# Cross-attention and a routed mixture of experts on one core: weight pieces, early loads, and where the empty tiles stand

## The reference

```python
x = x + xattn(layernorm(x), ctx, Wq, Wg, bg, Wkv, Wo)
#   q = fm(query @ Wq.T), k = fm(kv @ Wk.T), v = kv @ Wv.T, 16 heads; fm(t) = t+1 if t>0 else exp(t)
#   kv_summary = sum over s of k v^T, z = 1/(q . k_sum + eps)
#   out = (q kv_summary z) * sigmoid(query @ Wg.T + bg) @ Wo.T
x = x + ffn(layernorm(x), Wr, We, be)
#   logits = x @ Wr (8 experts); top 2, softmax over the two
#   out = sum over experts e of gate_e * (x @ We[e] + be[e])
```

## Time and profile before

| what | us |
|---|---|
| median of three timed runs | 557.02 |
| the profiled execution, its own time | 559.25 |
| its span, from first to last instruction | 557.7 |
| first 100 us: start, keys and queries of batch 0 | 100 |
| three like stretches of 97 us (to 391.3) | 291.3 |
| expert tiles and the tail | 166.4 |

### The profile page before, as it was taken

One profiled execution on the slowest core, in us unless ns is written; L12 is line 12 of the kernel. 1 busy time (PEld: TensorE's weight loads), 2 busy tenths in 40 slices (PEclk: granted clock), 3 DMA queues, 4 the chain that ended last, 5 costly groups with the idle time before them and its releaser, 6 DMA issues.

```text
span 557.7 us, 12238 instructions
## 1 busy us (share of the span) xinstructions
PE 523.0 (94%) x4084; PEld 424.3 (76%) x4084; DVE 305.6 (55%) x918; ACT 209.7 (38%) x372; POOL 211.8 (38%) x235
## 2 busy tenths in 40 slices
PE   6999999899999999999999999999998879998990
PEld 5777788687778888777887878788876658886880
DVE  4483248637533773753377375377677675443440
ACT  6455432343443234344323444432442234333330
POOL 5342346521566032256603125300133563544353
PEclk9999999999999999999999999999999989999996
DMA  8912943551464225146422513679897988756855
GB/s 265 392 60 79 300 143 130 187 196 74 138 209 134 93 81 203 60 141 206 148 78 96 202 46 119 214 261 365 278 274 232 256 166 167 153 105 116 167 68 65
DMA packets 40873, 92.93 MB, mean 167 GB/s; under 512 B 4784, under 2 KB 4784, under 8 KB 40688
## 3 DMA queue, kind: packets, MB, share of 16 engines
q0 software_dynamic: 15184, 42.56, 28.7%
q1 hardware_dynamic: 24336, 47.22, 25.4%
q10 hardware_dynamic: 1296, 2.40, 1.3%
HBM read 53.81 MB, written 40.18 MB: 169 GB/s over the span
## 4 chain that ended last, share of the span: by engine, by line
PE 55%; DMA 16%; issue 7%; POOL 4%; POOLq 3%; DVE 1%; ACTq 1%; ACT 1%; DVEq 0%
PE pj L1133 15%; PE pj L1135 15%; PE pj L1134 15%; DMA out_dram<-khat,out_idx 8%; DMA out_dram<-buf,out_idx 6%; PE tp L1125 5%; PE pj L1220 2%; PE kvb L1192 2%; POOL aux L517 1%; DMA wraw<-in_L_ffn_We_dram 1%; POOLq L587 1%; POOL out_dram L592 1%; POOLq L586 1%; DMA we_halves<-aux 1%; PE pj L1142 1%
## 5 line engine op out<-in xcount | busy, mean ns | idle before, releaser
L1133 PE MATMUL pj<-R 128*128 128x512 f32 x448 | 184.5, 412 | 2.2 <-DVE R L794 2.2
L1135 PE MATMUL pj<-R 128*128 128x512 f32 x448 | 176.6, 394 | 0.0
L1134 PE MATMUL pj<-R 128*128 128x512 f32 x448 | 175.5, 392 | 0.0
L1133 PEld LDWEIGHTS pj<-R 128*128 128x128 f32 x448 | 84.9, 190 | 19.0 <-DVE R L794 3.8
L1135 PEld LDWEIGHTS pj<-R 128*128 128x128 f32 x448 | 84.6, 189 | 19.2
L1134 PEld LDWEIGHTS pj<-R 128*128 128x128 f32 x448 | 85.0, 190 | 15.3
L1133 PE MATMUL pj<-R,aux 128*128 x156 | 66.1, 424 | 9.5 <-DVE aux L798 4.5
L1135 PE MATMUL pj<-R,aux 128*128 x156 | 62.4, 400 | 0.0
L1134 PE MATMUL pj<-R,aux 128*128 x156 | 62.0, 397 | 0.0
L859 DVE SCALAR_TENSOR_TENSOR khat<-buf,khat 128x512 f32<-128x512 f32 x32 | 23.9, 747 | 59.2 <-ACT buf L663 57.6
L794 DVE TENSOR_TENSOR R<-tp,R 128x512 fp32r<-128x512 f32 x64 | 43.4, 683 | 16.4 <-ACT R L624 16.4
(11 more groups left out here) (198 smaller groups left out, 714.7 us busy)
## 6 DMA issues: line engine op xcount, KB each, us to landing
we_halves<-aux POOLq DMA_DIRECT2D x28, 512.0 KB, 4.7
R<-we_halves SPq DMA_DIRECT2D x6, 2048.0 KB
buf<-xs SPq DMA_DIRECT2D x34, 264.0 KB
buf<-in_ctx_dram SPq DMA_DIRECT2D x15, 512.0 KB, 4.5
wraw<-in_L_ffn_We_dram POOLq DMA_DIRECT2D x14, 512.0 KB, 5.6
wraw<-in_x_dram SPq DMA_DIRECT2D x4, 1024.0 KB, 8.7
out_dram<-gate SPq DMA_DIRECT2D x4, 1024.0 KB, 5.3
xs<-zeros POOLq DMA_DIRECT2D x4, 594.0 KB, 8.3
```

Of the source, the lines that this page charges most:

```text
L1133: nc.tensor.matmul(bank[:, :], s_hi(k), m_hi(k), start=(k == 0), stop=False)
L1134: nc.tensor.matmul(bank[:, :], s_hi(k), m_lo(k), start=False, stop=False)
L1135: last = nc.tensor.matmul(bank[:, :], s_lo(k), m_hi(k), start=False, stop=(k == KT - 1))
```

## The change

It has five parts.

1. Start: `ctx_pair(0, 1)` is issued ahead of the weights Wq, and the small loads (router weights, bias) behind `ctx_pair(0, 2)`; DVE waits for them at the first gate in place of before the first keys. The idle product on PE is 512 columns wide in place of 256.
2. Pieces: each 2 MB transfer of expert weights becomes four of 512 KB. For expert 6 each piece waits for the one before. Expert 7's low half comes in two pieces of 512 KB; its high half comes in four of 256 KB, issued one at a time between the loads of tiles 9, 10 and 11. The store of the last batch's x2 is four stores of a quarter, behind the loads of tiles 11 to 14.
3. Scales: in POOL's loop the four `scale` of x2 stand before the first cut, and the third cut stands behind the `scale` of x.
4. Plan: the tiles without rows stand last (tiles 35 to 38 rather than 17 to 20 for these inputs), with expert 7.
5. Two vector instructions of the plan fall away.

```diff
@@ sync
+            def store_last(t):
+                sp.wait_ge(SEMS["x2"], nth("x2", B - 1, t))
+                sp.dma_start(out_rows[(B - 1) * L + t * P:(B - 1) * L + (t + 1) * P, :], x2[:, t, :]).then_inc(x2_stored, 16)
...
-            sp.dma_start(wr_sb[:, :, :], ...)
-            sp.dma_start(bias[:, :], ...)
+            ctx_pair(0, 1)
             load_w(WQ)
-            ctx_pair(0, 1)
             load_w(WG)
...
             ctx_pair(0, 2)
+            sp.dma_start(bias[:, :], ...)
+            sp.dma_start(wr_sb[:, :, :], ...)
...
-            def load_halves(e):
+            def load_halves(e, one_by_one=False):
                 sp.wait_ge(wx_stored, 32 * 2 * e)
-                sp.wait_ge(we_ready, 16 * e)
-                sp.dma_start(R[:, 2 * e:2 * e + 2, :, :]..., wx_dram[e, :, :, :]...).then_inc(we_ready, 16)
+                sp.wait_ge(we_ready, 64 * e)
+                both_ = R[:, 2 * e:2 * e + 2, :, :].rearrange("p a k d -> p (a k) d")
+                for q in range(4):
+                    if q and one_by_one:
+                        sp.wait_ge(we_ready, 64 * e + 16 * q)
+                    sp.dma_start(both_[:, 2 * q:2 * q + 2, :].bitcast(F32),
+                                 wx_dram[e, 2 * q:2 * q + 2, :, :].rearrange("a p d -> p a d")).then_inc(we_ready, 16)
+            def load_last_low():
+                for q in range(2):
+                    sp.dma_start(R[:, 2 * E - 2, 2 * q:2 * q + 2, :].bitcast(F32), ...).then_inc(half_loaded, 16)
+            def load_last_high(q):
+                sp.wait_ge(we_ready, 64 * (E - 1) + 16 * q)
+                sp.wait_ge(half_loaded, 32)
+                sp.dma_start(R[:, 2 * E - 1, q, :].bitcast(F32), wx_dram[E - 1, KT + q, :, :]).then_inc(we_ready, 16)
...
-            load_halves(6)
-            load_half(7, 1)
-            for m in range(XS + 5, M0):
+            load_halves(6, one_by_one=True)
+            load_tile(9)
+            load_last_high(0)
+            load_last_high(1)
+            load_tile(10)
+            load_last_high(2)
+            load_last_high(3)
+            for m in range(11, M0):
                 load_tile(m)
-                if m == XS + 6:
-                    store_x2(B - 1)
+                if m < 11 + TT:
+                    store_last(m - 11)
@@ gpsimd, loop over batches
                 load_expert_at(2 * b + 2, 1)
+                for t in range(TT):
+                    scale(1, t, 1, "_x2", b, t)
                 cut_to_dram(2 * b + 2, 0)
                 load_expert_at(2 * b + 3, 0)
                 cut_to_dram(2 * b + 2, 1)
                 load_expert_at(2 * b + 3, 1)
-                for t in range(TT):
-                    scale(1, t, 1, "_x2", b, t)
-                cut_to_dram(2 * b + 3, 0)
                 scatter(b, 0)
                 scatter(b, 1)
                 scale(0, 0, TT, "_x", b + 1, 0)
+                cut_to_dram(2 * b + 3, 0)
                 scatter(b, 2)
@@ vector
                         if i == 0:
+                            if b == 0:
+                                dve.wait_ge(small_loaded, 32)
...
-                link(nc.vector.tensor_scalar(last_t[:, :], last_t[:, :], 1.0, float(M1), ALU.mult, ALU.subtract))
-                link(nc.vector.tensor_scalar(iota_r[:, :], iota_t[:, :], last_t[:, 0:1], None, ALU.add))
...
-                big, more = tiles_of(tmp, M0, M1, iota_r)
+                big, more = tiles_of(tmp, M0, M1, iota_t)
...
-                link(nc.vector.tensor_scalar(tile_t[:, :], iota_r[:, :], 0.0, float(E * ROWS), ALU.is_lt, ALU.mult))
+                link(nc.vector.tensor_scalar(tile_t[:, :], iota_t[:, :], last_t[:, 0:1], float(E * ROWS), ALU.is_ge, ALU.mult))
...
-            dve.wait_ge(small_loaded, 32)
             dve.wait_ge(consts, N_CONSTS)
@@ tensor
-            idle_product(D // 2)
+            idle_product(D)
...
-                pe.wait_ge(we_ready, 16 * e + 16)
+                pe.wait_ge(we_ready, 64 * e + 64)
```

More of the change, by code:

```diff
@@ L334, in _ @@
             load_w_chunks(WV)
-            sp.dma_start(wr_sb[:, :, :], wr.rearrange("(k p) e -> p k e", p=P)).then_inc(small_loaded, 16)
-            sp.dma_start(bias[:, :], bg.rearrange("(a d) -> a d", a=1).broadcast_to((P, D))).then_inc(small_loaded, 16)
+            ctx_pair(0, 1)
             load_w(WQ)
-            ctx_pair(0, 1)
             load_w(WG)
@@ L344, in _ @@
             ctx_pair(0, 2)
+            sp.dma_start(bias[:, :], bg.rearrange("(a d) -> a d", a=1).broadcast_to((P, D))).then_inc(small_loaded, 16)
+            sp.dma_start(wr_sb[:, :, :], wr.rearrange("(k p) e -> p k e", p=P)).then_inc(small_loaded, 16)
             ctx_pair(0, 3)
@@ L1018, in plan_rest @@
                 at = 2 * M1 * E
-                iota_r, tile_u, tile_o = [tmp[:, at + i * M1:at + i * M1 + M1] for i in range(3)]
+                tile_u, tile_o = [tmp[:, at + i * M1:at + i * M1 + M1] for i in range(2)]
                 bound, first, last, flag, ends = [tmp[:, at + 3 * M1 + i * (E + 1):at + 3 * M1 + (i + 1) * (E + 1)] for i in range(5)]
@@ L1056, in plan_rest @@
                 yield
-                link(nc.vector.tensor_tensor(tile_t[:, :], iota_r[:, :], tile_o[:, :], ALU.add))
+                link(nc.vector.tensor_tensor(tile_t[:, :], iota_t[:, :], tile_o[:, :], ALU.add))
                 flag_tiles(ends, bound, big, more, tile_u)
```

16 lines of the change are left out of this document (5 added, 11 removed).

## The result

The changed kernel took 561.97 us (median of 11 runs, 559.96 to 564.63) against 557.11 us (11 runs, 555.77 to 563.55) for the kernel before in the same comparison: ratio 1.0073, 95% interval 1.0044 to 1.0102. Forecast were 541.9 us and a range from 536.5 to 549.5. The forecast was wrong in sign and in size.

A forecast was written before the change was run, and what follows sets the result against it. It took PE to bound the first phase and adds the last stretch. Terms -0.8 - 2.9 + 0.9 - 12.3 = -15.1 us took the profiled 559.25 to 544.2; 2.2 lower for the median gave 541.9, range 536.5 to 549.5.

The forecast's parts named there:

- from sooner adds to a sooner end of the expert stage: Expert tiles: adds set the pace from tile 17, its add comes at 475, so the stage ends 12.3 us sooner.
- the cost of the moved cuts: Rounds, `keys`: moved cuts hold DVE instructions, 0.3 us a round, 0.9 in all, range 0 to 10.
- the end of the range (-1.7): Start: context pair ahead of Wq removes a 0.80 us stall; -0.8 us, from -1.7 to +0.1.
- The stops of 1.66 and 1.23 us: Batch 0: two PE stops with one cause, removed by putting the scales first; -2.9 us, to -1.5.
- a rival at 547 us: Rounds: cuts collide with DVE in `keys`, two hits in each of 3 rounds, 5 to 6 us; chance 0.12.
- the 6.5 of the sum: Expert tiles: with at most 512 KB ahead, adds from tile 5 on come 6.5 us sooner.
- a stop for the late loads of tiles 9 to 11: Expert tiles: tile 11's load, issued at 437, lands at 441.5; a new PE stop of about 3 us.
- The first rival: Expert tiles: SP's eight steps take 5.5 to 6 us, stage gains only 5.3; 548.9 us, chance 0.17.
- The tail: End of the span: 13.3 us from the issue of tile 34's add to the end.
- rivals 1 and 2: One: late expert loads, 548.9 us, chance 0.17. Two: cuts collide in `keys`, 547 us, chance 0.12.
- rival 3: Last expert tiles: the plan does not shorten the tail, or adds stop PE more often; about 552 us, chance 0.08.
- The mechanism that I gave for "slower": SP's queue: tile 11's load behind seven waits, slower from 7.3 us each, about 570 at 8.82; chance 0.03.

The follow-up runs named there:

- c_last: The kernel before with part 3 alone, but the third cut behind scatters 2 and 3; ratio 0.9963 to the kernel before.
- p_only: The kernel before with part 2 alone (the pieces); ratio 1.0011 to the kernel before.
- c_both: The kernel before with part 3 alone, whole: scales first and third cut moved; ratio 1.0017 to the kernel before.
- a_stores_late: The changed kernel with the third cut's two stores issued behind scatters 2 and 3, its copy and subtraction still ahead; ratio 0.9999 to the kernel before.
- after_again: The changed kernel, unaltered, run again on another chip; ratio 1.0098 to the kernel before.
- c_both2: The kernel before with part 3 alone, whole, run again on a second chip; ratio 1.0075 to the kernel before.
- sc: The kernel before with parts 1 and 3 alone (start and scales); ratio 1.0063 to the kernel before.
- pc: The kernel before with parts 2 and 3 alone (pieces and scales); ratio 1.0088 to the kernel before.
- a_third_mid: The changed kernel with the third cut between scatter 2 and scatter 3; ratio 1.0135 to the kernel before.
- a_third_last: The changed kernel with the third cut behind scatters 2 and 3, ahead of the fourth; ratio 0.9923 to the kernel before.
- a_third_last2: The changed kernel with the third cut behind scatters 2 and 3, measured once more on another chip; ratio 0.9928 to the kernel before.
- a_third_back: The changed kernel with the third cut put back ahead of scatter 0, scales still first; ratio 1.0003 to the kernel before.
- a_split: The changed kernel with GpSimd's subtraction of a cut in eight steps of 128 columns; ratio 1.0013 to the kernel before.

## Why the forecast was wrong, point by point

The forecast put the end of the span at 542.6 us (544.2 less 1.55); it came at 558.8. Of the 16.2 us between them, 11.1 are parts 2 and 4 (-12.3 forecast, -1.2 measured) and 6.2 are the rounds (-2.0 forecast, +4.2 measured); the start gave 1.1 more than forecast. So two steps failed: from sooner adds to a sooner end of the expert stage, and the cost of the moved cuts.

**Part 1, the start: right.** No stop near 19 us; the first product of k v^T comes at 78.80 and not 80.67. That is 1.9 us in this pair, beyond the end of the range (-1.7); over all profiles it is 1.0: in the 12 with part 1 that product comes at 78.9 us on average (78.2 to 79.7), in the eight without at 79.9 (79.2 to 80.7).

**Part 3, what it removes: right.** The stops of 1.66 and 1.23 us are gone in every kernel with the scales first, and c_last shows their worth (2.1 us timed, the 3.1 us between a first round of 99.5 and one of 96.4 in its profile and that of p_only).

**Part 3, what it costs: this step failed.** The text put the delay of `norm_x` at 0 to 1 us a round, and took 0.3 a round in the sum, 0.9 us in all. It was 2.3 a round, 6.9 in all. The upper end of 10 us covered it, but I took a value near the lower end. Why was that wrong? I argued that DVE has slack in `keys` (53.19 of 97.06 us) and that one cut there costs nothing. Both are true and beside the point: two of the three held instructions of a round cost nothing, but the third, at 151.53 in the view above, stands on the short path from a key product through ACT and DVE to PE's next low half, and there it met late signals, for which the text had no term. The runs show both prices apart. In the third round of c_both, on another chip, the signals are on time and the same instruction is held, beside the copy of the fourth cut:

```profile
346.46 2.07 DVE L859 SCALAR_TENSOR_TENSOR khat<-buf,khat 128x512 f32<-128x512 f32 x1 [2.45 <-ACT buf L663]
```

PE has no stop of 0.6 us in that round, and it takes 96.7 us for the 96.3 of p_only on that chip. Late signals alone stop PE for 0.6 to 0.8 us (a_stores_late). Both together stop it for 1.8 to 2.3 us in every round of the changed kernel, after_again, c_both2, sc and pc. Averaged slack of an engine says nothing of an instruction that PE waits for. And I counted the moved cut as 5 us of GpSimd's time, and not what it does to the work behind it: it closes the gap between scatters 2 and 3 and sets the fourth cut's subtraction at exactly that instruction.

The rule that I had weighed, the exclusion of a DVE instruction with two SBUF inputs and a GpSimd instruction (the Trainium skill, SBUF — State Buffer, Who interferes with whom), is borne out: the nine DVE rows of 1.3 us and more in the changed kernel's rounds are all of that kind, and none is left when the subtraction is cut into short steps. The text's remark that L893 "ends as it ends" is not so: it ends at 98.58, the subtraction at 98.03, and the 0.55 us between them are about one run of L893, as after a wait for the whole subtraction. The other two of the changed kernel's first round, 0.16 us long elsewhere:

```profile
117.22 1.97 DVE L848 TENSOR_TENSOR w_top<-egap,w_top 128x1 f32<-128x1 f32 x1
...
139.46 2.25 DVE L843 TENSOR_TENSOR members<-both 128x8 bf16<-128x8 f32 x1
```

I had this as a rival at 547 us with a chance of 0.12. Its fixed 5 to 6 us came near the 6.2 measured in the rounds; that signals of PE come late was in none of the rivals.

**Part 2, the pieces: half right, and its step from the adds to tile 17 failed.** The adds do come sooner: that of tile 8 at 51.8 us behind tile 0's transposes in place of 55.9, 4.1 us for the 6.5 of the sum (52.8 and 55.5, so 2.7, on average over 12 profiles with the pieces and eight without). By tile 17 nothing is left: 88.6 in place of 87.8, 88.5 and 88.6 on average. Tile 17's transposes come 71.5 us after tile 0's with the pieces (68.2 to 74.4), 71.1 without (68.3 to 71.8). The text's own next term was a stop for the late loads of tiles 9 to 11. The load times were right: tile 11's stands at 436.42, for the 437 of the text. Expert 6's four pieces take 19.6 us, from the first issue at 404.1 to the last landing at 423.7, where the text had 18, and 21 by the fixed cost that it took from the Trainium skill (DMA: Bandwidth & Descriptors, Anatomy of one DMA); that section gives it for transfers that GpSimd issues, and these are issued by SP.

```profile
420.69 0.36 SPq L364 DMA_DIRECT2D buf<-xs  x1
...
430.17 0.17 DVE L834 COPY lg<-pj 128x8 f32<-128x8 f32 x1 [3.91 <-remote]
...
433.48 0.79 PE L1149 MATMUL pj<-R,aux 128*128 x1 [2.70 <-DVE aux L815]
...
436.42 0.24 SPq L364 DMA_DIRECT2D buf<-xs  x1
...
438.04 0.66 PE L1216 MATMUL tp<-ident,buf 128*128 128x128 f32 x4
...
441.29 0.58 ACT L728 CAST aux<-tp 128x512 fp32r<-128x512 f32 x1 [7.05 <-remote]
...
445.71 0.60 PE L1216 MATMUL tp<-ident,buf 128*128 128x128 f32 x4
```

But in the changed kernel's profile PE never waits for them. By the packed trace the loads of tiles 9, 10 and 11 have landed at 424.9, 432.9 and 441.4; PE transposes these tiles at 438.0, 441.3 and 445.7, each time with no idle time ahead. Tile 9 is already 4.6 us late (41.4 us behind tile 0 and not 36.8): DVE gets the logits about 4 us late, ACT stands behind it, PE stops for 2.70 us and its granted clock falls (mean 0.78 from 430.12 to 438.04). These are the late signals again. sc, which has no pieces, is as late at tile 9 (41.2). In four other kernels with the pieces (pc, a_third_mid, a_third_last, a_third_last2) PE does stop for such a load, by 2.1 to 2.7 us in all. So the early adds are eaten by late signals in some profiles and by late loads in others; how much each takes over many executions is not shown. The first rival (0.17) had the effect, "tile 17's add stays near 482", and not the mechanism: SP's steps did not take 5.5 to 6 us throughout, or tile 11's load would have been later.

**Part 4, the plan: the step from adds to an end failed.** I wrote that the adds, and not PE, set the pace behind tile 17, because 18 adds took 57.1 us and PE's need was 54.4. But PE is busy 69.73 of the 72.33 us between tiles 17 and 38 before, and 69.12 of 73.56 after. It works through all 39 tiles, empty or not, in either order. The adds only kept time with it, as far as these stretches show: no run made the adds behind tile 17 faster by themselves. With the empty tiles last, the stretch to tile 38 takes 73.6 to 75.6 us, with them at 17 to 20 it takes 71.7 to 74.6; behind tile 38 come 16.2 in place of 18.9 to 19.9. From tile 17 to the end of the span it is 90.8 us on average in 11 profiles with the new plan (89.8 to 91.8) and 92.1 in nine with the old (91.0 to 93.5): 1.3 us, timed 2.3. The sum had 12.3 for parts 2 and 4 together. The tail was also undersized: each empty tile's add still waits for one before it, so tile 38's comes 9.3 us behind tile 34's, and 6.9 us end the span: 16.2 for 13.3.

**The rivals.** They were written as if one excluded the others. Here the effects of rivals 1 and 2 came together, and half of rival 3. Put end to end with the text's own numbers: 544.2 in the profiled execution, plus 7 for tile 17's add at 482, plus 6 for the cuts, plus 3 for the tail is 560.2; the profiled execution took 560.4. Measured, the terms are 8.0, 6.2 and 2.9, less 1.1 for the start, so that they meet within 0.2 us is luck; that they add up is not. The mechanism that I gave for "slower", seven waits of 7.3 us on SP's queue, did not happen.

**A version that beats both.** a_third_last: 553.5 and 554.0 us against 558.0 and 557.9 of before, 0.7 to 0.8% faster, and by the ratios 1.5 to 1.8% faster than the changed kernel.

## What to carry to other kernels

When a long step moves on an in-order queue, look at what it is now ahead of, and ask for each of those whether two engines wait for its effect: here a buffer that is read by the scatter and then written by ACT, and a subtraction that holds the DVE instruction with two SBUF inputs that it meets. Put such a step behind the last short one that others wait for, even if that leaves it back to back with its neighbour. A chain of adds (or stores) that advances at the pace of the main engine is not shown to be the bound by its pace: compare the busy time of the main engine in the same stretch first. And where several rivals can hold at once, give the case that they add up, and let the range reach it.

## What the runs showed of the hardware that I had not expected

**PE's signals can come 2 to 4 us late while PE goes on.** In the changed kernel's timeline above, ACT reads the key product at 150.41 and has, without idling, the value product at 151.85; but the value product comes after the key product on PE and takes 3.0 us there (148.27 to 151.29 by PE's rows). So the key product was done 1.5 us or more before ACT was told, and the semaphore events given above say 2.3. Idle time of 0.9 us and more with releaser "remote" stands before ACT's cast or reading in all three rounds of six kernels (changed, after_again, c_both2, sc, pc, a_stores_late), before DVE's copy of the logits in the three rounds of a_third_back (2.1 to 2.9 us, there behind scatters 0 and 1), and in no round of the other 13. The changed kernel has it in the expert tiles too (the rows at 430.17 and 441.29 shown with part 2).

All seven have GpSimd's cut right ahead of scatters, which then are issued in a row. But c_both on the other chip and a_split have four in a row as well, and their signals in the rounds are on time or 1.2 us late at most; and the stores in front of the scatters are not needed (a_stores_late). Lateness also goes with the chip. In the packed traces of the six kernels on chips 5 and 12, no semaphore of PE moves more than 0.6 us after PE's record, neither in the three rounds nor in tiles 0 to 17; in the 14 others, the kernel before among them, some move 1.1 us late or more. c_both shows 0.17% of loss and none late on chip 5, c_both2, the same kernel, 0.75% and up to 3.7 us late on chip 6. The changed kernel itself was not run on chip 5 or 12. What holds the signals stays open. No run here shifted the scatters alone by a microsecond.

**Chips differ in the undisturbed round.** Without a stop it is 96.3 to 96.4 us on the chips of the first and the last comparison of the experiments (5 and 12) and 97.0 to 97.3 on the two between (6 and 1) and in the first profile of before, at a granted clock of 1.00 everywhere. c_both lost 0.17% on the former and 0.75% on one of the latter. An effect that hangs on a meeting of two engines within 1 us has to be measured on more than one chip.
